# Layer 3 of a fused four-layer network: loop over batches written out, expert rows summed by TensorE, rounding shared with ScalarE, gathers moved ahead of the key/value build

## The reference, cut to what matters

```python
contrib = gathered * (flat_g * keep)[:, None]            # four expert rows for each token, times their gates
x = x + shared + sum_k(contrib)                          # x before layer 3
x = x + L3_xattn(ctx, ctx, layernorm(x), mask)           # 16 heads, 77 context tokens, then @ w_out.T + b_out

n = layernorm(x)                                         # L3_ffn, 256 -> 1024 -> 256
h = act_quant(n) @ weight_quant(w1).T
h = silu(depthwise_conv3(h) + conv_b)
x = x + act_quant(h) @ weight_quant(w2).T

def act_quant(x):
    scale = 127.0 / clip(max(abs(x), axis=-1), 1e-5)
    return clip(round(x * scale), -128, 127) / scale
```

## Time and profile before

| what | us |
|---|---|
| median of 3 runs | 3358.77 |
| lowest and highest of them | 3352.96, 3365.67 |
| the profiled execution | 3362.81 |
| its span, first to last instruction | 3361.3 |
| layers 0 to 2 and the experts, in it | 2508 |
| preparation of layer 3 | 65.6 |
| the four turns | 197.4, 197.8, 195.2, 197.3 |

### The profile page before, as it was taken

The page is one execution under the profiler, slowest core; times in us unless marked ns, Lnnn a source line. Parts: engine busy times, 40 slices in busy tenths (PEclk is TensorE's granted clock), DMA queues, the critical chain, the costliest instruction groups (busy, mean ns, idle before and its releaser), DMA issues. The chain is left out here.

```text
span 3361.3 us, 42650 instructions
## 1 busy us (share of the span) xinstructions
PE 2357.2 (70%) x15958; PEld 1931.5 (57%) x15958; DVE 2137.3 (64%) x4737; ACT 1338.6 (40%) x2178; POOL 982.0 (29%) x734
## 2 busy tenths in 40 slices
PE   0757657567558999999849999999972436354453
PEld 0535435345347788888749999999971323233232
DVE  1766676657665666666535666666647577675857
ACT  0424434234244655565424444544531233233223
POOL 1212222132132244444440000000005644546464
PEclk9968868678679999999969999999995768687686
DMA  8200000000010011100023343343423101011110
GB/s 304 80 0 27 1 1 27 1 14 14 0 40 1 1 40 39 39 27 21 17 76 111 129 139 111 131 138 109 134 91 94 51 14 41 28 34 50 34 50 12
DMA packets 158116, 191.02 MB, mean 57 GB/s; under 512 B 23394, under 2 KB 122599, under 8 KB 157930
## 3 DMA queue, kind: packets, MB, share of 16 engines
q1 hardware_dynamic: 144106, 157.21, 14.3%
q0 software_dynamic: 13824, 31.35, 3.0%
HBM read 123.50 MB, written 71.43 MB: 58 GB/s over the span
## 5 line engine op out<-in xcount | busy, mean ns | idle before, releaser
L2004 POOL DMA_INDIRECT picked<-expert_out,so x160 | 159.9, 999 | 813.1 <-DMA so<-slots 765.3
L204 PE MATMUL SC<-Xhi,Whi 128*128 128x320 f32 x1024 | 320.4, 313 | 7.1 <-DVE Wlo L1882 5.3
L204 PE MATMUL SC<-Xlo,Whi 128*128 128x320 f32 x1024 | 317.5, 310 | 0.0
L204 PE MATMUL SC<-Xhi,Wlo 128*128 128x320 f32 x1024 | 317.4, 310 | 0.0
L1118 POOL TENSOR_TENSOR ff_Hlo<-ff_HF,ff_Hhi 128x512 fp32r<-128x512 f32 x112 | 147.9, 1321 | 421.3 <-ACT ff_Hhi L1251 421.2
L322 POOL TENSOR_TENSOR PR<-PR,rs 128x616 f32<-128x616 f32 x128 | 153.6, 1224 | 326.2 <-DVE rs L292 326.2
L204 PEld LDWEIGHTS SC<-Xhi,Whi 128*128 128x128 f32 x1024 | 193.4, 189 | 7.8 <-DVE Wlo L1882 5.7
L204 PEld LDWEIGHTS SC<-Xlo,Whi 128*128 128x128 f32 x1024 | 193.5, 189 | 0.0
L204 PEld LDWEIGHTS SC<-Xhi,Wlo 128*128 128x128 f32 x1024 | 193.2, 189 | 0.0
L1901 DVE TENSOR_TENSOR Hlo<-HF,Hhi 128x320 fp32r<-128x320 f32 x256 | 125.4, 490 | 104.2 <-ACT Hhi L1859 104.2
L1882 DVE TENSOR_TENSOR Wlo<-Wraw,Whi 128x1024 fp32r<-128x1024 f32 x96 | 114.6, 1223 | 119.2 <-ACT Whi L1847 119.2
(11 more groups left out here) (456 smaller groups left out, 7014.0 us busy)
## 6 DMA issues: line engine op xcount, KB each, us to landing
expert_in<-zeros SPq DMA_DIRECT2D x4, 5120.0 KB, 32.2
rowsin<-expert_in SPq DMA_DIRECT2D x32, 640.0 KB, 5.9
expert_out<-rowsout SPq DMA_DIRECT2D x32, 640.0 KB, 4.0
Wraw<-L_wg SPq DMA_DIRECT2D x32, 512.0 KB, 7.2
Wraw<-L_wu SPq DMA_DIRECT2D x32, 512.0 KB, 7.2
Wraw<-L_wd SPq DMA_DIRECT2D x32, 512.0 KB, 7.8
Xin<-x SPq DMA_DIRECT2D x10, 512.0 KB, 4.6
Xin<-x_after_l SPq DMA_DIRECT2D x10, 512.0 KB, 4.2
```

Source lines behind the costliest of these rows:

```text
L204: last = nc.tensor.matmul(out, lhs[l], rhs[r], start=start and n == 0, stop=stop and n == 2)
L2004: nc.gpsimd.indirect_dma_start(picked[g][:, t, k, :], None, oute[:, :], bass.IndirectOffsetOnAxis(ap=so[g][:, t, k:k + 1], axis=0)).then_i ...
```

## The change

It writes the four batches out as straight code in one block with the preparation, so that the semaphores count on through all batches and nothing is cleared between them. The constants `EARLY` and `PH` go.

- The sum of the expert rows moves to TensorE. ScalarE writes the gates onto diagonals (`gates_on_diagonal`, 16 activations of 128x128 for each group, into storage that `XT` and `OT` have done with), TensorE multiplies them with `picked` (`combine`, 16 matmuls of 128x256 for each group), VectorE adds the result to the tokens and takes their statistics (`take_combined`) ahead of its last step of the batch before. POOL's weighing and adding (lines 1996 and 1999) go, and so do VectorE's in the preparation.
- Layer norm is applied by ScalarE (`apply`; VectorE computes one more small operation, `nm`), and so is the rounding of the normalized input (`scale_up`).
- The maximum over the chunks is taken in two halves (`chunk_maximum`): the first after chunk 5 of the loop, the second behind it, and a `max` of the two.
- In the rounding of the hidden values POOL has no part. VectorE scales both halves of the chunks and rounds the upper one; ScalarE adds `MAGIC` to the lower one and takes it off both. No clip at 127 stands in the lower half.
- POOL issues the 32 gathers of the next batch right behind its part of the attention, without waiting for the value product, and builds `Kbd` and `Vbd` after them. The last batch gathers nothing.

The diff, cut to its core (the helpers of the attention are unchanged):

```diff
@@ POOL, for each batch
+                    def gathers(g, c):
+                        pool.wait_ge(sm["slots_in"][g], 16 * (c + 1))
+                        if c:
+                            pool.wait_ge(sm["c_psum"][g], c)
+                        for t in range(TT):
+                            for k in range(K2):
+                                nc.gpsimd.indirect_dma_start(picked[g][:, t, k, :], None, oute[:, :],
+                                                             bass.IndirectOffsetOnAxis(ap=so[g][:, t, k:k + 1], axis=0)).then_inc(gathered[g], 16)
+                    for b in range(B):
+                        for g in range(G):
+                            add_bias(g, b)
+                        attention_pool(nc, pool, T, sm, b)
+                        if b + 1 < B:
+                            for g in range(G):
+                                gathers(g, b + 1)
+                        if b + 1 < B:
+                            for g in range(G):
+                                pool.wait_ge(sm["ot_psum"][g], UNITS * (b + 1))
+                            pool.wait_ge(ctx_in, CTX_IN * (b + 2))
+                            keys_and_values(nc.gpsimd).then_inc(kv_ready, 1)
-                        keys_and_values(nc.gpsimd)
-                        for g in range(G):
-                            for t in range(TT):
-                                gather(g, t, range(EARLY, K2))
...
-                            link(weigh(nc.gpsimd, g))
-                            for k in range(K2):
-                                link(add_picked(nc.gpsimd, g, k))
-                        combine(0)
-                        for g in range(G):
-                            pool.wait_ge(s2_ready, g + 1)
-                            v = SL[:, NHC - PH:, g * TOK:(g + 1) * TOK]
-                            nc.gpsimd.tensor_tensor(v, v, bc_at(S2B[:, g * TOK:(g + 1) * TOK], 1, PH), ALU.mult).then_inc(pooled, 1)
-                        combine(1)
@@ ACT
+                        if c and g == 1:
+                            for i in range(G):
+                                act.wait_ge(sm["y_psum"][i], c)
+                        for t in range(TT):
+                            for k in range(K2):
+                                last = nc.scalar.activation(diag[g][:, t * K2 + k, :], ident[:, :], ACT.Copy, scale=gk3[g][:, t, k:k + 1])
...
+                        attention_act(nc, act, T, sm, b, GP, 1.0 / D ** 0.5)
+                        if b + 1 < B:
+                            for g in range(G):
+                                gates_on_diagonal(g, b + 1)
+                        for g in range(G):
+                            root(g, 2 * b + 2)
+                        for g in range(G):
+                            apply(g, 2 * b + 2, T["X"][g])
+                        for g in range(G):
+                            scale_up(g, b)
...
+                            act.wait_ge(sm["scaled"][g], b + 1)
+                            nc.scalar.activation(low, low, ACT.Identity, bias=magic[:, :]).then_inc(sm["raised"][g], 1)
+                            act.wait_ge(sm["rounded"][g], b + 1)
+                            nc.scalar.activation(SQ[:, HALF:, tok], high, ACT.Identity, bias=nmagic[:, :]).then_inc(sm["q_ready"][g], 1)
+                            act.wait_ge(sm["raised"][g], b + 1)
+                            nc.scalar.activation(SQ[:, 0:HALF, tok], low, ACT.Identity, bias=nmagic[:, :]).then_inc(sm["q_ready"][g], 1)
@@ PE, between the scale and the second product
+                        if b + 1 < B:
+                            for g in range(G):
+                                pe.wait_ge(sm["s2_ready"][g], b + 1)
+                                combine(g, b + 1)
@@ DVE
+                    def take_combined(g, c):
+                        dve.wait_ge(sm["x_in"][g], 16 * (c + 1))
+                        dve.wait_ge(sm["c_psum"][g], c + 1)
+                        x = Xin[g][:, :, :].rearrange("p t d -> p (t d)")
+                        tt(x, x, GP[g][:, :], ALU.add).then_inc(sm["c_taken"][g], 1)
+                        dve.wait_ge(sm["c_taken"][g], c + 1)
+                        ln_stats(g, Xin[g])
...
+                            if h == HALF + 1:
+                                for i in range(2):
+                                    dve.wait_ge(sm["s_ready"][i], b * HALF + HALF // 2)
+                                for g in range(G):
+                                    last = chunk_maximum(S2B, 0, g)
+                                link(last)
...
-                            mine, pools = SL[:, 0:NHC - PH, tok], SL[:, NHC - PH:, tok]
-                            link(tt(mine, mine, bc_at(S2B[:, tok], 1, NHC - PH), ALU.mult))
-                            tsc(mine, mine, MAGIC, MAGIC + 127.0, ALU.add, ALU.min).then_inc(rounded, 1)
-                            dve.wait_ge(pooled, g + 1)
-                            tsc(pools, pools, MAGIC, MAGIC + 127.0, ALU.add, ALU.min).then_inc(rounded, 1)
+                            low, high, by = SL[:, 0:HALF, tok], SL[:, HALF:, tok], bc_at(S2B[:, tok], 1, HALF)
+                            dve.wait_ge(sm["s2_ready"][g], b + 1)
+                            tt(low, low, by, ALU.mult).then_inc(sm["scaled"][g], 1)
+                            link(tt(high, high, by, ALU.mult))
+                            tsc(high, high, MAGIC, MAGIC + 127.0, ALU.add, ALU.min).then_inc(sm["rounded"][g], 1)
+                        if b + 1 < B:
+                            for g in range(G):
+                                take_combined(g, b + 1)
@@ loop
-        with nc.Fori(0, B) as b:
-                sa.rezero()
+                    for b in range(B):
...
+            sa.rezero()
```

More of the change, by code:

```diff
@@ L1938, in layer_3 @@
         T = {}
-        for name, shape in (("X", [P, TT, D]), ("XN", [P, TT, D]), ("XT", [P, KC, TOK]), ("OT", [P, KC, TOK]),
+        diag = []
+        for name in ("XT", "OT"):
+            both = sb("L3" + name, [P, G * KC, TOK])
+            T[name] = [both[:, g * KC:(g + 1) * KC, :] for g in range(G)]
+            diag.append(both[:, :, :].rearrange("p k n -> p (k n)").rearrange("p (i n) -> p i n", n=P))
+        for name, shape in (("X", [P, TT, D]), ("XN", [P, TT, D]),
                             *((f"PR{i}", [P, HH, CTXP]) for i in range(NPR)), ("PT", [P, 2, BLK, P]), ("stats", [P, TT, 6]),
-                            ("mv", [P, TT, 2]), ("sd", [P, TT]), ("rstd", [P, TT]), ("nw", [P, TT]), ("mx", [P, HH]),
+                            ("mv", [P, TT, 2]), ("sd", [P, TT]), ("rstd", [P, TT]), ("nw", [P, TT]), ("nm", [P, TT]), ("mx", [P, HH]),
                             *((f"rs{i}", [P, HH]) for i in range(NPR))):
@@ L2105, in _ @@
+                        take_combined(g, 0)
+                    for b in range(B):
                         for g in range(G):
-                            sp.dma_start(so[g][:, :, :].rearrange("p t k -> p (t k)"), slotv[bass.ds(nextb, 1), g].squeeze(0)).then_inc(sm["slots_in"][g], 16)
+                            ln_rstd(g, 2 * b + 1)
+                        attention_dve(nc, dve, T, sm, b, link, SC)
                         for g in range(G):
-                            sp.dma_start(gk3[g][:, :, :].rearrange("p t k -> p (t k)"), gatev[bass.ds(nextb, 1), g].squeeze(0)).then_inc(sm["gates_in"][g], 16)
+                            dve.wait_ge(sm["y_psum"][g], b + 1)
+                            dve.wait_ge(sm["x_bias"][g], b + 1)
+                            x = T["X"][g][:, :, :].rearrange("p t d -> p (t d)")
+                            tt(x, x, GP[g][:, :], ALU.add).then_inc(sm["y_taken"][g], 1)
+                            dve.wait_ge(sm["y_taken"][g], b + 1)
+                            ln_stats(g, T["X"][g])
@@ L2245, in _ @@
[L2245 to L2262 removed]
+                            dve.wait_ge(sm["xn_ready"][g], 2 * b + 2)
@@ L2266, in _ @@
                             link(nc.vector.reciprocal(sx[g][:, :], am[g][:, :]))
[L2267 removed]
+                            tsc(sx[g][:, :], sx[g][:, :], 127.0, None, ALU.mult).then_inc(sm["sx_ready"][g], 1)
                             link(tsc(isx[g][:, :], am[g][:, :], 1.0 / 127.0, wm1[:, :], ALU.mult, ALU.mult))
[L2269 to L2272 removed]
+                        for g in range(G):
+                            dve.wait_ge(sm["xr_ready"][g], b + 1)
                             for t in range(TT):
```

437 lines of the change are left out of this document (232 added, 205 removed).

## The result

The changed kernel took 3311.05 us (median of 4 runs, 3307.0 to 3315.02) against 3355.86 for the kernel before: a ratio of 0.9863, with a 95% interval of 0.9836 to 0.9891. It is faster, by a third of what was forecast: 44.8 us in place of 132. The profiled execution took 3315.02 us, its span is 48.0 shorter than before.

What follows compares the result with a forecast made beforehand. The prediction saw no engine as the bound but a chain of hand-overs standing still at the loop's turn, the rounding and the gathers. Gains of 132.1 us from 3362.8 gave 3230.7, median 3226; own range 3211 to 3241, wide 3198 to 3262.

Steps and rivals of the forecast that it cites:

- three turns: From VectorE's last step of a batch to the next attention operation: 9.6 us against 17.6, gain 8.0, three times: 24.
- four roundings: Rounding of hidden values, from its start (T0) to the last step's end: 36.4 us becomes 23.4, four times: 52.
- chunk 0 of the last batch: First hidden chunk's release to ScalarE, with no gathers or diagonals in that batch: at 2861.9, gain 20.8 us.
- chunk 0 of batches 0 to 2: First hidden chunk's release to ScalarE, after the earlier burst: 2873.5 in place of 2882.7, 9.2 us each, 27.6.
- part 3: Gathers moved right behind attention, and second norm: chunk 0 released earlier, gaining 27.6 us in batches 0 to 2, 20.8 in the last.
- rival (d): Instruction supply: TensorE's code after attention held until the burst ends, 99 us more, exposed fetches 67 more: 3392; chance 0.03.
- Theory A: From the experiments, not the forecast: a burst holds every TensorE release until some 4.7 us after its last gather.
- Rival (a): Chunk 0's late release came of the loop, or the earlier burst no longer meets it: 3203 us; chance 0.14.
- (b): Lateness belongs to TensorE's first hidden chunks, whatever POOL does; last batch 12 us later than forecast: 3251 us; chance 0.14.
- Part 1: Turn of the loop between batches: barrier goes, six small VectorE operations of 0.16 us each; gain 8.0, three times: 24.
- Parts 2 and 5: Rounding of hidden values without POOL, gain 13.0 us four times: 52; and preparation, first attention operation at 2575.6, gain 10.9.
- Part 4: Chunk maxima in two halves, the first pushing the chunk loop: a loss of 0.8 us, four times: 3.2.

Runs made afterwards that it cites:

- n0: Changed kernel without the gathers of batches 1 to 3 (batch 0's rows used again), on a late chip: 3209.02 us, 0.9545 of the kernel before.

## Why the prediction was wrong

Term by term, from the two profiled executions of the first comparison, forecast and measured:

| term | forecast | measured |
|---|---|---|
| preparation, first attention operation 2575.6 | 10.9 | 9.6 (2576.94) |
| three turns, 17.6 to 9.6 | 24 | 16.8 (12.3, 11.9, 11.9) |
| four roundings, T0+36.4 to T0+23.4 | 52 | 50.2 (T0+23.8, 24.7, 25.1, 20.8) |
| maxima | -3.2 | +3.3 |
| chunk 0 of the last batch | 20.8 | 20.6 |
| chunk 0 of batches 0 to 2 | 27.6 | -52.8 (19.5, 17.5, 15.8 later, from the first attention operation) |
| sum | 132.1 | 47.7 |

**The step that failed is part 3**, by 80 of the 84 us that are missing. It turned two late chunks into a rule, that a release in the *second half* of a burst comes 3.95 us after it, and so moved the burst under the attention's end without a price. The end of the rule was near (in the three batches the first release behind the burst came 4.7, 5.4 and 0.7 us after the last gather), the beginning was not: releases were late from 0.7 us after the first gather on. The value products and the output product had never stood in a dense burst in the trace of before, but for one half of the output product 1 to 2 us into one, and their chain to chunk 0, which the prediction itself puts at 22 us and more, then starts behind the burst. I should have priced that they are held: the first half came 36, 33 and 17 us late, the second 29, 25 and 28.

The figure did stand in the text: rival (d) has 33 us of chain starting at 2873.5, 99 us in all, with 0.03. Its cause was another. Among the packets of the instruction queues there are some in every batch, but none between 2629.6 and 2739.8, where batch 0 stands still; nothing was held for them, and its further 67 us did not come. Theory A has its price without its cause, and that is how (d) should have been asked: what if anything of TensorE's is held, not only its code. Rival (a) ("not of the gathers") falls with n0, and (b) ("TensorE's first chunks, whatever POOL does") with batch 3.

What neither the sum nor a rival held: that the lateness goes with the chip. On a prompt chip the terms without part 3 make 10.9 + 24 + 52 - 3.2 = 83.7, and the measured gain there is 3288.30 - 3205.35 = 83.0. That they agree to 0.7 is in part luck, as the same terms as measured in the table make 79.9. And the 3205 us of a prompt chip, though within the prediction's wide range, would not have borne part 3 out: the gain is 83 and not 132, as the kernel before has nothing to recover there. The kernel before pays for its four bursts as well: it is 3356 on one kind and 3285 on the other, 17.6 us a burst, near the 12 to 14 of chunk 0 and the few of the transposes ahead of it. That share is from the times alone; the kernel before was not traced on a prompt chip.

**Part 1** had the right steps but one wrong size, in the turns: 12.3 in place of 9.6. POOL's bias add was called harmless, as nobody waits for it early. It starts 1 us after DVE's last step, and beside it two of the six small operations take 2.12 and 2.27 us in place of 0.16: 4.1 us in all, more than the 2.7 that the first turn lacks (3.8 in the first turn of the prompt chip). The Trainium skill, "SBUF — State Buffer", section "SBUF: two separate sides", has VectorE and GpSimd shut each other out of a shared port; the trace agrees for these two: each ends within 0.02 us of the end of a bias add, of which one takes 2.3 us. The other half of what that section of the Trainium skill says, weighed in part 3 (VectorE keeps GpSimd from writing descriptors), shows in the preparation, where the gathers run beside VectorE's rounding of the weights:

```profile
2529.61 1.29 DVE L2320 TENSOR_SCALAR SL<-SL,ws 128x2048 f32<-128x2048 f32 x1
2529.96 2.31 POOL L2078 DMA_INDIRECT picked<-expert_out,so  x1 [0.31 <-issue]
```

This gather and the two behind it take 2.22 to 2.31 us in place of 0.95, and the kernel before has the same three at 2.13 to 2.28, which the prediction passed over when it called the one of 5.04 the only sign of the rule; a longer burst would also have made its sum 9 us lower, not higher. Within the bursts of batches 1 to 3 the rule cost nothing: beside eight memsets of 4096 columns, and beside the `tensor_scalar` of 256 on a prompt chip, the gathers kept their pitch of 1.25 us.

**Parts 2 and 5** came out as worked out: multiplications 2.29, clip 1.23, ACT's passes 1.99, the step without POOL at T0 + 23.8. The diagonals took 0.30 each (forecast 0.33). **Part 4** was a gain: the first halves fit into the loop.

**Left open:** which part of the late chips holds the release; whether it is the chip or a passing state of it (only one late chip was used twice, 17 minutes apart, late both times); whether it takes indirect gathers or any transfer that GpSimd issues, as a plain one of its was not tried; why in the kernel before the first transposes, 13 us into a burst, were prompt, while in the changed one the last transposes of the attention were late 0.7 us into it; and at what rate of gathers a late chip lets the releases through.

## What to carry to other kernels

Long unbroken runs of indirect gathers on GpSimd can hold back what TensorE releases, and by tens of us, so they do not belong beside a chain of short hand-overs; dealt out, with 0.5 us of other work before each, they cost 13 us on a late chip where the dense ones cost 101. A wait whose releaser has no name is a mechanism that one does not know: price it at the full length of what runs beside it, from its first instruction on. And where the kernel before is 2% quicker on another chip, ask first what differs between the chips before two versions are compared across them.

## What the runs showed of the hardware

- The five chips fall into two kinds: on two of them TensorE's releases are up to 36 us late during a dense run of indirect gathers, on three no release is late in any of the traces, with the same gathers at the same pitch of 1.25 us. It is worth 105 us to the changed kernel and 71 to the one before.
- The late kind also shows in the records of the gathers' semaphore updates: 267 of 1536 in the changed kernel's trace, 1332 with the gathers paced, all 1536 on prompt chips.
- On the late chips it is not the traffic (the same 4 MB a batch by plain transfers: 3208 us) and not VectorE's being idle, and it gives way to 0.5 us of GpSimd's other work ahead of each gather.
- Beside a bias add of 2.34 us on GpSimd a VectorE operation on 4 columns lasts 1.8 to 2.3 us in place of 0.16, on both kinds.
- Beside VectorE's `tensor_scalar` of 2048 columns an indirect gather takes up to 2.3 us on GpSimd in place of 0.95; beside a memset of 4096 columns it does not lengthen.
